# Convolution taps as diagonal matmuls, four norms scaled on VectorE, a split last FFN, and a new instruction order

## The chip, the cores and the metric

The kernel runs on 1 core of one Trainium2 chip. The metric is the device time of one execution in microseconds (us). Matmuls are TensorE (PE), elementwise work and reductions are VectorE (DVE), activations and copies are ScalarE (ACT), small elementwise work and masks are GpSimd (POOL); SyncE (SP) issues all DMAs.

## What is computed

One pre-norm decoder layer over 8 sequences of 256 tokens with 128 channels, in float32:

```python
x = x + linear_attention(layernorm(x), Wqkv, Wproj) + bproj     # 16 heads of 8, elu+1 feature map
x = x + causal_softmax_attention(layernorm(x), ctx, Wq, Wk, Wv, Wo)
x = x + ffn(layernorm(x))
# ffn(h): scores = sigmoid(h @ Wr); top 2 of 8 experts, weights cw normalised
#   experts 0..3: (silu(h@Wg) * (h@Wu)) @ Wd;  4 and 6: h;  7: relu(h);  5: nothing
#   routed = sum of cw * expert;  shared = causal depthwise convolution of h over 4 tokens + conv_b
#   return routed + shared
```

## The kernel before

Each of the 8 sequences is a "batch" of 256 tokens, held as two token tiles of 128 (T = 2). A batch passes through three stages. The self stage (names `self_*`, `xn`, `phiq`, `kvsum`, `o`) ends in `x1`. The cross stage builds three bfloat16 parts each of q and k, sends them by DMA into stacked tiles `qs` and `ks`, finds the row maxima (`max`, six units for a batch, each read by one DVE `reduce` of 128x1024), then computes the scores again (`soft`), exponentiates them on ACT (`exp`), masks on POOL and multiplies by the values (`pv`); it ends in `x2`. The FFN stage normalises (`norm3`), transposes (`ffn_x_t`), routes (`route`, ten small DVE instructions), multiplies by gate and up (`ffn_gate_up`), forms the hidden values (`gate`, `times_up` on DVE, `hid` on POOL), transposes them (`ffn_hid_t`), copies them (`hidT` on ACT), and multiplies by down (`ffn_down`); `finish` on DVE adds `base` and `store_out` writes 128 KB.

A layer norm goes through three engines: DVE computes mean and variance (`stats`, `var`, L686 and L697), POOL computes `vareps`, `negmean`, `rstd` and `shift` (L488 to L497, four instructions), and ACT writes `xn = x * rstd + shift`, one instruction for each token tile (L565).

The convolution has four taps. POOL computes the last one with its bias (`conv`, L529); DVE adds the other three (`tap`, L840, 128x256 each, both inputs in SBUF); `ffn_down` adds the sum on PE with one matmul by the identity for each token tile.

The order of all work is written out by hand: a table `ORDER` gives for each engine a list of words `step.batch.argument`, and every engine runs its list strictly in that order, waiting on semaphores. Stages of several batches are interleaved in it: around one word of batch 7's softmax stand words of the FFN of batches 4 and 5. `BANKS` says which PSUM bank each stay uses. `warm.b.n` puts n float32 128x128 matmuls by the identity on PE whose result nobody reads; 18 more stand at the start. Nineteen such matmuls stand in the PE list after the last `max` words. `clear` (eight DVE memsets of 128x1024) prepares `ks` and `qs`; `heads`, `causal`, `picks` and others on POOL prepare constants.

## Time and profile before

| | |
|---|---|
| time, median of 3 runs | 182.6 us (182.4 to 182.61) |
| the profiled execution | 182.75 us, of which its span, first to last instruction, is 181.0 us |
| busy: PE / DVE / ACT / POOL | 94% / 89% / 71% / 65% of the span |
| DVE reductions of the scores | 48 of 1.22 us, from 30.3 to 143.7 us |
| last result written by DVE, end of the span | 178.7 us, 181.0 us |
| granted TensorE clock | 1.00 in every stretch |

Read it in three stretches. Until 30 us the self stage of the first batches runs and the constants are made. From 30 to 144 us the reductions run, six for a batch. From 144 us on only softmax, `pv` and the FFNs of the last batches are left; the time ends with batch 7's store. A matmul's duration in the trace contains its pipeline, so successive matmuls overlap, and the distance from start to start says more than the duration. One float32 matmul stands as two records.

### The profile page before, as it was taken

How to read it: one execution, taken by the hardware profiler on the slowest of the kernel's cores; microseconds unless marked ns; L12 is line 12 of the kernel's file. 1: busy time of each engine (PE TensorE's matmuls, PEld its weight loads, DVE VectorE, ACT ScalarE, POOL GpSimd, SP SyncE). 2: the span in 40 equal slices, each digit the busy share in tenths (PEclk: the TensorE clock that was granted, in tenths of full speed). 3: DMA queues.
4: the chain of work that ended last, by engine and by line, in shares of the span. 5: the costliest groups of instructions: out<-in, count | busy, mean ns of one | idle time of the engine just before them, and what ended most of it. 6: DMA issues, size and time to landing. Idle time of an engine off the chain costs nothing. (4 is left out here: it accounts for less than half of the span.)

```text
span 181.0 us, 5282 instructions
## 1 busy us (share of the span) xinstructions
PE 169.6 (94%) x1898; PEld 119.3 (66%) x1898; DVE 160.6 (89%) x448; ACT 127.8 (71%) x289; POOL 118.3 (65%) x248
## 2 busy tenths in 40 slices
PE   6889999989999999999999999989989899999993
PEld 6856788757666767656765687457646647756593
DVE  6897789999997998899999998999799879979992
ACT  1469988687788958977978679488564878663540
POOL 6768887764686757758846358468457577757541
DMA  5781023311323122123322122142000010000001
GB/s 175 222 320 41 5 61 81 89 50 45 78 61 91 40 55 63 46 59 81 85 57 63 33 51 71 38 107 87 2 4 0 5 31 4 2 29 4 29 2 58
...
## 3 DMA queue, kind: packets, MB, share of 16 engines
...
q14 instruction: 10, 0.08, 0.2%
...
## 5 line engine op out<-in xcount | busy, mean ns | idle before, releaser
L752 DVE TENSOR_REDUCE negmax<-max_pair 128x4 f32<-128x1024 f32 (+1 forms) x48 | 58.4, 1217 | 4.3 <-PE max_pair L862 3.8
L622 ACT ACTIVATE probs<-soft_pair 128x1024 f32<-128x1024 f32 x48 | 49.3, 1026 | 12.9 <-PE soft_pair L862 12.7
L521 POOL TENSOR_SCALAR_AFFINE_SELECT probs<-probs 128x512 f32<-128x512 f32 (+1 forms) x48 | 37.6, 796 | 15.6 <-ACT probs L622 15.6
L862 PE MATMUL pv_bank<-probs,vs 128*32 128x256 f32 (+1 forms) x448 | 21.1, 329 | 0.1
L862 PE MATMUL soft_pair<-qs,ks 64*128 64x256 bf16 (+1 forms) x256 | 18.8, 245 | 0.4 <-DMA qs<-maxparts 0.3
L536 POOL TENSOR_TENSOR hid<-hraw,cw 128x256 f32<-128x256 f32 x16 | 10.5, 661 | 12.9 <-DVE cw L806 10.7
L495 POOL TENSOR_TENSOR rstd<-vareps,exponent 128x2 f32<-128x2 f32 x24 | 17.5, 728 | 2.0
L862 PE MATMUL max_pair<-ks,qs 64*128 64x128 bf16 (+1 forms) x256 | 18.4, 242 | 0.0
L862 PEld LDWEIGHTS pv_bank<-probs,vs 128*32 128x32 f32 x448 | 12.8, 109 | 7.2 <-issue 1.7
L862 PE MATMUL max_pair<-causal,picks 64*128 64x128 bf16 (+1 forms) x192 | 15.2, 237 | 1.6 <-DVE negmax L752 0.8
L565 ACT ACTIVATE xn<-inputs,shift,rstd 128x128 f32<-128x128 f32 x32 | 14.1, 492 | 3.1 <-POOL shift L497 3.1
L862 PE MATMUL ffn_bank<-inputs,x3T 128*128 128x8 f32 (+1 forms) x46 | 15.3, 429 | 0.0
L862 PEld LDWEIGHTS soft_pair<-qs,ks 64*128 64x128 bf16 x256 | 8.2, 94 | 9.8 <-ACT probs L622 4.0
L840 DVE SCALAR_TENSOR_TENSOR conv<-x3T,inputs,conv 128x256 f32<-128x256 f32 x24 | 14.4, 602 | 0.1
L862 PE MATMUL max_pair<-ident 128*128 128x128 f32 x74 | 12.1, 315 | 1.6 <-POOL ident L416 1.6
L862 PEld LDWEIGHTS max_pair<-causal,picks 64*128 64x128 bf16 x192 | 6.6, 94 | 8.3 <-DVE negmax L752 4.6
L862 PEld LDWEIGHTS max_pair<-ident 128*128 128x128 f32 x74 | 11.0, 227 | 1.6 <-POOL ident L416 1.6
L862 PE MATMUL cross_bank<-inputs 128*128 128x128 f32 (+1 forms) x48 | 10.9, 336 | 0.6 <-DVE krest L741 0.6
L488 POOL TENSOR_SCALAR vareps<-mv 128x2 f32<-128x2 f32 x24 | 5.1, 211 | 8.3 <-DVE mv L697 7.0
L862 PEld LDWEIGHTS max_pair<-ks,qs 64*128 64x128 bf16 x256 | 9.8, 94 | 0.4
L547 POOL TENSOR_TENSOR base<-skip,relu 128x256 f32<-128x256 f32 x8 | 5.8, 726 | 5.2 <-DVE skip L832 4.9
L862 PEld LDWEIGHTS cross_bank<-inputs 128*128 128x128 f32 x48 | 6.7, 190 | 2.6 <-issue 1.1
...
## 6 DMA issues: line engine op xcount, KB each, us to landing
...
qs<-maxparts SPq DMA_DIRECT2D x32, 4.0 KB
...
```

The source lines that it names most:

```text
L488: nc.gpsimd.tensor_scalar(t["vareps"][:, :], t["mv"][b.par][:, :, 1], 1.0, 1e-5, ALU.mult, ALU.add).then_inc(vareps_done[n], 1)
L495: nc.gpsimd.tensor_tensor(t["rstd"][b.par][:, :], t["vareps"][:, :], exponent[:, :], ALU.pow).then_inc(rstd_done[n], 1)
L521: nc.gpsimd.affine_select(out=v, in_=v, compare_op=ALU.is_ge, fill=0.0, base=0, pattern=[[0, n], [1, P]], channel_multiplier=-1).then_inc( ...
L536: nc.gpsimd.tensor_tensor(hid[b.par][:, t, :].rearrange("p (e i) -> p e i", e=EM), hid0[:, t, :].rearrange("p (e i) -> p e i", e=EM), cw[b ...
L547: nc.gpsimd.tensor_tensor(base[b.par][:, :, :], skip[b.par][:, :, :], relu7[b.par][:, :, :], ALU.add).then_inc(base_done, 1)
L565: nc.scalar.activation(t["out"][b.par][:, i, :], source(n, b)[:, i, :], ACT.Identity, scale=t["rstd"][b.par][:, i:i + 1], bias=t["shift"][ ...
L622: nc.scalar.activation(probs[b.par][g][:, k, :], soft_pair[:, :], ACT.Exp).then_inc(exp_done, 1)
L752: nc.vector.tensor_reduce(maxima, max_pair[:, :].rearrange("p (u h k) -> p u h k", u=2, h=n), AX.X, ALU.max, negate=True).then_inc(max_rea ...
L840: nc.vector.scalar_tensor_tensor(out=conv[b.par][:, :], in0=x3T[b.par][:, j:j + S], scalar=w["conv"][:, j:j + 1], in1=conv[b.par][:, :], o ...
L862: return nc.tensor.matmul(out, lhsT, rhs, start=start, stop=stop, skip_group_check=True)
```

## The change

1. **Norms on DVE.** For norm 1 of batches 0 and 1 and norm 3 of batches 6 and 7, POOL computes only `vareps` and `rstd`, and DVE writes `xn = (x - mean) * rstd`, two instructions of 128x128 (`centre`). ACT's two instructions go away for them.
2. **Taps on PE.** For batches 6 and 7 the three DVE taps go away. ACT makes three diagonal matrices once (`diagonals`), and `ffn_conv` puts for each token tile one matmul by the identity and three by the diagonals on PE, ahead of `ffn_down`, into the bank of down's result.
3. **The last FFN by token tile.** For batch 7 `ffn_hid_t`, `hidT`, `ffn_down`, `finish` and `store_out` run once for each token tile, in banks of their own.
4. **Another order.** The lists of all five engines are rearranged. 8 `warm` matmuls instead of 19 stand at the end of PE's list, and 4 new ones stand in its beginning. On SP the two loads of the router bias move from behind `lo_q.0.0` to ahead of `lo_k.0.0`.
5. A few waits are added or moved (`act_q` waits for `phiq` two batches back, `x2` for `skip` two batches back).

```diff
+XN_ON_VECTOR = {1: (0,1), 2: (), 3: (6, 7)}
+LAST = B - 1
+CONV_ON_PE = (6, 7)
 ORDER = {
...
-        self_x_t.0.0 self_q1.0.0 cross_k.0.0 self_kv.0.0 self_x_t.1.0 cross_v.0.0 self_sum.0.0 self_q1.1.0 self_out.0.0
+        self_x_t.0.0 self_q1.0.0 warm.0.1 cross_k.0.0 warm.0.1 self_kv.0.0 cross_v.0.0 self_x_t.1.0 self_sum.0.0
...
-    "cross_bank": "cross.0 cross.1 cross.2 cross.3 cross.4 cross.5 cross.6 cross.7 pv.6",
+    "cross_bank": "cross.0 cross.1 cross.2 cross.3 cross.4 cross.5 cross.6 cross.7 pv.6 down.6",
-    "soft_high": "self.4 soft.all up.6",
+    "soft_high": "self.4 soft.all up.6 downb.7",
-    "max_high": "max.all",
+    "max_high": "max.all down.7",
...
                 def go(b, _):
+                    direct = b.c in XN_ON_VECTOR[n]
                     pool.wait_ge(mv_done[n], b.count(2, 2))
...
-                    nc.gpsimd.tensor_scalar(t["negmean"][:, :], t["mv"][b.par][:, :, 0], -1.0, 0.0,
-                                            ALU.mult, ALU.add).then_inc(vareps_done[n], 1)
+                    if not direct:
+                        nc.gpsimd.tensor_scalar(t["negmean"][:, :], t["mv"][b.par][:, :, 0], -1.0, 0.0,
+                                                ALU.mult, ALU.add).then_inc(vareps_done[n], 1)
...
+                    if direct:
+                        return
...
+            def centre(n):
+                t = norm[n]
+
+                def go(b, _):
+                    dve.wait_ge(rstd_done[n], b.count(1, 1))
...
+                    for i in range(T):
+                        nc.vector.scalar_tensor_tensor(out=t["out"][b.par][:, i, :], in0=source(n, b)[:, i, :],
+                                                       scalar=t["mv"][b.par][:, i, 0:1],
+                                                       in1=t["rstd"][b.par][:, i:i + 1].to_broadcast([P, C]),
+                                                       op0=ALU.subtract, op1=ALU.mult).then_inc(xn_done[n], 1)
...
+            def spread_taps(_, __):
...
+                for j in range(KC - 1):
+                    nc.scalar.activation(diagonals[:, j, :], ident[:, :], ACT.Identity, scale=w["conv"][:, j:j + 1]).then_inc(diagonals_done, 1)
...
+            def ffn_conv(b, _):
...
+                for t in range(T):
+                    o = half_down(b, t)
+                    mm(o, conv[b.par][:, t * P:(t + 1) * P], ident[:, :], start=t == 0 or b.c == LAST, stop=False)
+                    for j in range(KC - 1):
+                        mm(o, x3T[b.par][:, j + t * P:j + (t + 1) * P], diagonals[:, j, :], start=False, stop=False)
+
+            def ffn_down(b, half):
+                pe.wait_ge(hidT_done, b.count(1, half + 1))
...
+                for t in [half] if b.c == LAST else range(T):
+                    o = half_down(b, t)
                     for i in range(2):
...
-            def finish(b, _):
+            def finish(b, t):
...
+                if b.c == LAST:
+                    nc.vector.tensor_tensor(result[b.par][:, t, :], half_down(b, t), base[b.par][:, t, :], ALU.add).then_inc(result_done, 1)
+                    return
```

Lines of the changed kernel are higher by some 30 to 90: L734 there is L686 before (`stats`), L747 is L697 (`var`), L721 is L673 (`clear`), L880 and L887 are L813 and L820 (`gate`, `times_up`), L905 is L840 (`tap`), L852 to L873 are L785 to L806 (`route`), L931 is L862 (matmuls), L1142 and L1148 are L1073 (`ffn_hid_t`), and L759 is `centre`.

DVE at the start, from the first statistics to the feature map of batch 0. Before:

```order
L686 BN_STATS stats1<-inputs 128x6 x2
L697 BN_AGGR mv1_0<-stats1 128x2 x2
L686 BN_STATS stats1<-inputs 128x6 x2
L697 BN_AGGR mv1_1<-stats1 128x2 x2
L673 MEMSET qs1 128x1024
L673 MEMSET ks2 128x1024
...
L741 SCALAR_TENSOR_TENSOR krest0<-cross_bank,kparts0 128x256
L703 SCALAR_TENSOR_TENSOR phiq0<-expq0,reluq0 128x256
L708 SCALAR_TENSOR_TENSOR phik0<-expk0,reluk0 128x256
```

Now:

```order
L734 BN_STATS stats1<-inputs 128x6 x2
L721 MEMSET qs1 128x1024
L747 BN_AGGR mv1_0<-stats1 128x2 x2
L721 MEMSET ks2 128x1024
L734 BN_STATS stats1<-inputs 128x6 x2
L759 SCALAR_TENSOR_TENSOR xn1_0<-inputs,mv1_0,rstd1_0 128x128 x2
L721 MEMSET qs2 128x1024
...
L806 SCALAR_TENSOR_TENSOR krest0<-cross_bank,kparts0 128x256
L747 BN_AGGR mv1_0<-stats1 128x2 x2
L759 SCALAR_TENSOR_TENSOR xn1_1<-inputs,mv1_1,rstd1_1 128x128 x2
L773 SCALAR_TENSOR_TENSOR phik0<-expk0,reluk0 128x256
```

One memset of 128x1024 now stands between the statistics and the variance of batch 0, one more before batch 1's statistics, and the two pairs that write `xn` stand among them; `phiq0` now comes later, before `kvsum0`.

DVE after the last statistics of batch 5, where batch 4 meets its gate. Before:

```order
L774 TENSOR_TENSOR x2_1<-pv_bank,inputs 128x256
L686 BN_STATS stats3<-x2_1 128x6 x2
L697 BN_AGGR mv3_1<-stats3 128x2 x2
L757 TENSOR_TENSOR maxparts1<-soft_pair,maxparts1 16x128
L813 SCALAR_TENSOR_TENSOR gated<-tang,ffn_bank 128x256
L785 SCALAR_TENSOR_TENSOR biased<-tanr0,rbias_all 128x2x8
L820 SCALAR_TENSOR_TENSOR hraw<-gated,ffn_bank 128x256
```

Now:

```order
L841 TENSOR_TENSOR x2_1<-pv_bank,inputs 128x256
L734 BN_STATS stats3<-x2_1 128x6 x2
L747 BN_AGGR mv3_1<-stats3 128x2 x2
L822 TENSOR_TENSOR maxparts1<-soft_pair,maxparts1 16x128
L852 SCALAR_TENSOR_TENSOR biased<-tanr0,rbias_all 128x2x8
L905 SCALAR_TENSOR_TENSOR conv0<-x3T0,inputs,conv0 128x256
L858 MAX best<-biased 128x8 x2
L880 SCALAR_TENSOR_TENSOR gated<-tang,ffn_bank 128x256
```

Three steps that do not need ACT's `tang` now stand ahead of the one that does.

DVE from the `x2` of batch 7 (`x2_1`) to the weights of batch 6. Before:

```order
L774 TENSOR_TENSOR x2_1<-pv_bank,inputs 128x256
L793 COPY match<-best 128x2x2
L686 BN_STATS stats3<-x2_1 128x6 x2
L697 BN_AGGR mv3_1<-stats3 128x2 x2
L813 SCALAR_TENSOR_TENSOR gated<-tang,ffn_bank 128x256
L840 SCALAR_TENSOR_TENSOR conv0<-x3T0,inputs,conv0 128x256 x2
L796 MATCH_REPLACE picked<-match,biased 128x14 x2
L820 SCALAR_TENSOR_TENSOR hraw<-gated,ffn_bank 128x256
```

Now:

```order
L841 TENSOR_TENSOR x2_1<-pv_bank,inputs 128x256
L734 BN_STATS stats3<-x2_1 128x6 x2
L747 BN_AGGR mv3_1<-stats3 128x2 x2
L880 SCALAR_TENSOR_TENSOR gated<-tang,ffn_bank 128x256
L852 SCALAR_TENSOR_TENSOR biased<-tanr0,rbias_all 128x2x8
L858 MAX best<-biased 128x8 x2
L860 COPY match<-best 128x2x2
L887 SCALAR_TENSOR_TENSOR hraw<-gated,ffn_bank 128x256
L759 SCALAR_TENSOR_TENSOR xn3_1<-x2_1,mv3_1,rstd3_1 128x128 x2
```

The taps are gone, routing of batch 6 has moved behind `x2_1`, and the norm of batch 7 is written here.

PE from the hidden transposes of batch 6 to the end. Before:

```order
L1073 MATMUL ffn_bank<-ident,hid0 128x128 x4
L862 MATMUL max_pair<-ident 128x128 x3
L862 MATMUL ffn_bank<-inputs,hidT0 128x128 x2
L862 MATMUL ffn_bank<-ident,conv0 128x128
...
L862 MATMUL max_pair<-ident 128x128
L1073 MATMUL max_pair<-ident,hid1 128x128 x4
L862 MATMUL max_pair<-ident 128x128 x5
L862 MATMUL max_pair<-inputs,hidT1 128x128 x2
L862 MATMUL max_pair<-ident,conv1 128x128
```

Now:

```order
L1148 MATMUL ffn_bank<-ident,hid0 128x128 x4
L931 MATMUL cross_bank<-ident,conv0 128x128
L931 MATMUL cross_bank<-diagonals,x3T0 128x128 x3
...
L931 MATMUL cross_bank<-inputs,hidT0 128x128 x4
L1142 MATMUL max_pair<-ident,hid1 128x128 x2
L931 MATMUL max_pair<-ident,conv1 128x128
L931 MATMUL max_pair<-diagonals,x3T1 128x128 x3
L931 MATMUL soft_pair<-ident,conv1 128x128
L931 MATMUL soft_pair<-diagonals,x3T1 128x128 x3
L1142 MATMUL soft_pair<-ident,hid1 128x128 x2
L931 MATMUL max_pair<-inputs,hidT1 128x128 x2
L931 MATMUL soft_pair<-inputs,hidT1 128x128 x2
```

The nine warm matmuls of this stretch have gone, and 16 matmuls of the convolution stand in it (4 of the old form went away).

## Rows read from the trace of the kernel before

**Rows 1.** The page's busy time: us, share of the span, instructions.
```profile
PE 169.6 (94%) x1898; PEld 119.3 (66%) x1898; DVE 160.6 (89%) x448; ACT 127.8 (71%) x289; POOL 118.3 (65%) x248
```

**Rows 2.** Windows: stretch, length, busy of PE, PEld, DVE, ACT, POOL, clock, DMA, GB/s.
```profile
0.00:13.00 13.00, 10.03 (x55) 8.61 (x55) 10.58 (x25) 5.42 (x13) 8.85 (x37) 1.00 0.73 245
13.00:30.00 17.00, 16.32 (x108) 13.36 (x108) 14.02 (x62) 15.13 (x47) 14.09 (x36) 1.00 0.17 43
30.00:150.00 120.00, 116.05 (x1517) 77.31 (x1512) 110.69 (x269) 92.05 (x196) 77.97 (x147) 1.00 0.21 54
165.00:181.00 16.00, 12.72 (x86) 10.00 (x84) 11.77 (x46) 5.67 (x15) 7.39 (x14) 1.00 0.08 26
```

**Rows 3.** Timeline, VectorE, start: start, us, instruction, idle before it.
```profile
5.79 0.91 DVE L673 MEMSET qs<- 128x1024 f32 x1 [0.16 <-DVE mv L697]
...
12.18 0.42 DVE L708 SCALAR_TENSOR_TENSOR phik<-expk,reluk 128x256 f32<-128x256 f32 x1
...
13.44 0.31 DVE L716 TENSOR_TENSOR kvsum<-self_bank,headmask 128x144 f32<-128x144 f32 x1 [0.17 <-PE self_bank L862]
```

**Rows 4.** Timeline, ScalarE and PE at the start, VectorE's first reduction.
```profile
6.40 0.88 ACT L565 ACTIVATE xn<-inputs,shift,rstd 128x128 f32<-128x128 f32 x2 [1.13 <-POOL shift L497]
...
7.63 0.38 PE L866 MATMUL self_bank<-ident,xn 128*128 128x128 f32 x2
...
30.29 1.23 DVE L752 TENSOR_REDUCE negmax<-max_pair 128x8 f32<-128x1024 f32 x1
```

**Rows 5.** Timeline, VectorE, the four long waits between 50 and 150 us.
```profile
56.25 1.23 DVE L752 TENSOR_REDUCE negmax<-max_pair 128x8 f32<-128x1024 f32 x1 [1.14 <-PE max_pair L862]
...
110.25 0.24 DVE L785 SCALAR_TENSOR_TENSOR biased<-tanr,rbias_all 128x16 f32<-128x16 f32 x1 [0.73 <-ACT tanr L644]
...
129.50 0.42 DVE L774 TENSOR_TENSOR x<-pv_bank,inputs 128x256 f32<-128x256 f32 x1 [0.67 <-PE pv_bank L862]
...
146.56 0.42 DVE L813 SCALAR_TENSOR_TENSOR gated<-tang,ffn_bank 128x256 f32<-128x256 f32 x1 [0.91 <-ACT tang L649]
```

**Rows 6.** The chain that ended last, batch 7's norm: start, us, what.
```profile
165.37 0.19 POOL vareps L488
...
165.65 0.42 POOL negmean L490
...
166.14 0.94 POOL rstd L495
...
167.16 0.20 POOL shift L497
...
167.39 0.89 ACT xn L565 x2
...
168.32 0.45 PE max_pair L866 x2
```

**Rows 7.** Timeline, PE and VectorE's last instruction, batches 6 and 7 to the end.
```profile
171.92 0.60 PE L1073 MATMUL ffn_bank<-ident,hid 128*128 128x128 f32 x4
...
173.20 0.71 PE L862 MATMUL ffn_bank<-inputs,hidT 128*128 128x128 f32 x4
...
174.64 0.39 PE L862 MATMUL max_pair<-ident 128*128 128x128 f32 x2
...
176.62 0.68 PE L862 MATMUL max_pair<-inputs,hidT 128*128 128x128 f32 x4
...
178.28 0.42 DVE L848 TENSOR_TENSOR result<-max_pair,base 128x256 f32<-128x256 f32 x1 [0.96 <-PE max_pair L862]
```

**Rows 8.** Taps and skips on VectorE: count, ns min/median/max, first and last start.
```profile
L840 DVE SCALAR_TENSOR_TENSOR conv<-x3T,inputs,conv x24: 446/480/1178, 83.2 to 176.0; 128x256 f32<-128x256 f32 x24
...
L832 DVE SCALAR_TENSOR_TENSOR skip<-xn,cskip,x x16: 327/344/779, 87.8 to 177.0; 128x128 f32<-128x128 f32 x16
```

**Rows 9.** Timeline, POOL and VectorE side by side in the tail.
```profile
174.94 0.72 POOL L547 TENSOR_TENSOR base<-skip,relu 128x256 f32<-128x256 f32 x1 [0.55 <-DVE skip L832]
174.98 1.49 DVE L840 SCALAR_TENSOR_TENSOR conv<-x3T,inputs,conv 128x256 f32<-128x256 f32 x2
```

305 lines of the change are left out of this document (174 added, 131 removed).

## The prediction

> **What bounds the kernel now.** I read the page's busy times first, then windows for three stretches, then the timeline around the waits, then the chain that ended last. The page [rows 1] shows PE at 94% and DVE at 89% of the span. A PE duration contains its pipeline, so PE's share overstates it; DVE's does not. The windows [rows 2] show where DVE has room: 2.4 us idle of 13 at the start, 3.0 of 17 from 13 to 30 us, 9.3 of 120 from 30 to 150 us, 4.2 of 16 at the end. So from 30 to 150 us DVE is busy 92% of the time, with 48 reductions among it that each need PE's scores first, and what counts there is how well two nearly full engines mesh. The largest single DVE waits of that stretch are four [rows 5]: 1.14, 0.73, 0.67 and 0.91 us, together 3.45 us, a third of the idle 9.3. In each of them DVE stands at an instruction whose input is late while others behind it could run. The end is another thing: the chain [rows 6] runs through batch 7's norm, from POOL's `vareps` at 165.37 to PE's transpose at 168.32 us, then through PE and DVE to `result` [rows 7]. The last result is written at 178.28 + 0.42 = 178.70 us and the span ends at 181.0, so the store takes 2.3 us, and 1.7 us of the 182.75 lie outside the span. The sum below is made against 182.75; the median of the runs shown is 182.6, 0.15 less, and I take 0.15 off at the end.
>
> **The start: late by 0.5 us (a gain of 0.3 to a loss of 1.3).** The norms of batches 0 and 1 leave ACT. What goes: POOL's `negmean` and `shift` (0.2 us each, as `shift` in [rows 6], with some 0.1 of hand-over each) and a pair on ACT of 0.88 [rows 4]. What comes: a pair on DVE of 128x128 with both inputs in SBUF. No such pair by that name exists before; the nearest row is `skip`, 0.33 at least, 0.34 in the median, 0.78 at most [rows 8], so a pair is 0.65 to 1.56, and 0.7 where POOL is quiet. Taken alone batch 0 would gain 0.6 + 0.2 = 0.8. But the order puts one memset of 0.91 plus 0.16 [rows 3] ahead of the variance of batch 0 and another ahead of `centre`. `xn` of batch 0 was done at 6.40 + 0.88 = 7.28 and PE took it at 7.63, behind its 18 warm matmuls [rows 4]. Now: variance one memset later, 4.75 + 1.07 = 5.8; `vareps` and `rstd` 1.1; `centre` waits for its place on DVE, behind the second memset and batch 1's statistics (5.8 + 1.1 + 0.5 = 7.4), and ends at 8.1. PE takes it at some 8.1 in place of 7.63: 0.5 late. Then DVE has, ahead of `kvsum` of batch 0, two pairs (1.4) more, and no wait of 0.17: on DVE alone `kvsum` (13.44 in [rows 3]) would be 1.3 late. Part of this is work that stood behind it anyway, and the 3.0 us that DVE idles from 13 to 30 us [rows 2] can take it up; but the chain of batch 0 to the first reduction at 30.29 [rows 4] is one of latencies, and most of its 0.5 stays. I take +0.5, the delay that PE sees first; 1.3 is DVE's whole delay, passed on; -0.3 is the case that batch 0 is late only where it would have waited later anyway and the reordered SP list pays (the two router loads now issue where SP waits for `lo_k`). The four new warm matmuls cost nothing as long as PE waits there for ACT; without that cover each is 0.26 (five in 1.32 us would be so by [rows 7], where they fill the gap up to 176.62), 1.0 in all, within the 1.3.
>
> **The middle: 0.9 us gained (3.0 gained to 1.5 lost).** The work stays the same: no instruction of the loops goes or comes but three short ACT instructions that make the diagonals, where ACT is busy 92.05 of 120 us [rows 2]; they hide there, and cost 3 x 0.44 (half of a pair in [rows 4]) if they do not. What changes is the order. At all four waits of [rows 5] other steps now stand ahead: the remainder of k for batch 4 and `x1` of batch 6 ahead of the reduction at 56.25; two taps of batch 2 ahead of `biased` at 110.25; two small steps of routing ahead of `x` at 129.50; routing, one tap and MAX ahead of `gated` at 146.56 (the second place shown). By size that is 0.8, 0.73, 0.3 to 0.67 and 0.9: up to 3.0 us. A filled hole pays only if DVE is what the next hole waits for, and every moved word opens holes that the trace of before cannot show. That PE is hardly ever idle either says that part of the time filled on DVE is spent waiting again later. I take a third, 0.9. The bounds are all of it, and half of it as a loss.
>
> **The end: 0.7 us gained (1.6 gained to 0.3 lost).** Batch 7's norm [rows 6]: `x2` of batch 7 waits for PE, as before. Variance is done at 165.29. Before, from there to `xn`'s end at 168.28 it takes 3.0. Now: hand-over and `vareps` 0.27; hand-over 0.08 and `rstd`, which took 0.94 here because a tap stood beside it, 0.70 or 0.94; `centre`'s pair 0.7, behind gate and three routing steps that are ready and short, with 0.05: 1.8 to 2.1, or 167.3. PE's matmuls of batch 5's down end there too. So PE's transpose starts 0.95 earlier, at 167.37. If the centre pair costs 1.56 it is 0.1 to 0.35 earlier; if nothing but the pair counted, 1.2.
> From there PE has one fixed list. Before, it went from the hidden transposes of batch 6 at 171.92 to the end of `result` at 178.70 in 6.8 us, nine of its matmuls being warm [rows 7]. Now, from 170.97: four transposes 0.44; a float32 matmul takes (174.64 - 173.20) / 6 = 0.24 from start to start [rows 7]; 8 of the convolution 1.92, 4 of down 0.96, two transposes 0.22, 8 of the convolution 1.92, two transposes 0.22, in sum 176.65; then ACT's copy of half the hidden values with its hand-overs 0.6 (down of the first tile runs under it, 0.48); two matmuls 0.48 and 0.15 to drain; `result` of one tile 0.3: 178.2. That is 0.5 before the 178.70, and 0.95 at 0.22 for a matmul, the smallest distance that down shows: I take 0.7. So PE gives back a part of what the norm wins: 16 matmuls in the place of 4 and 9 warm ones, but DVE, which must not be late, now has room. The six taps of batches 6 and 7 cost DVE some 3.4 us (six of the 24 in [rows 8], two of them the 1.49 of [rows 9]) and the two pairs bring 1.4; base and hidden values of batch 7 are needed by 176.1 and due near 175. If they were late by 1.0, the end would be a loss of 0.3. The store of half the size starts once its tile is done; SP's issue of the first half is over by then. I leave the 2.3 as they are, with no gain for the smaller size.
>
> **A rule weighed.** The taps have both inputs in SBUF. Beside a tap, POOL's `negmean` took 0.42 where `vareps` took 0.19 [rows 6], and beside POOL's `base` two taps took 1.49 where their median gives 0.96 [rows 8, 9]. The Trainium skill, page "SBUF — State Buffer", section "Who interferes with whom", says that a DVE instruction with two SBUF inputs contends with a GpSimd instruction that reads SBUF, and the later one waits for the earlier one to finish. The trace agrees. By that rule the change takes six such instructions away but makes the eight instructions of `centre` ones of the same kind, and ACT's form of the norm had no such trouble; what it would do is the rival "centre blocked" below.
>
> **The rivals.**
> *The holes were DVE's own.* DVE is the bound of the middle, and all 3.0 us come back. For it: 92% busy, and each hole has ready work behind it. Against: PE's idle is as small, and such gains seldom add up. 182.75 + 0.5 - 3.0 - 0.7 - 0.15 = 179.4 us.
> *Late start, slower.* The memsets and pairs ahead of batch 0's variance and `kvsum` push the whole chain, 1.3 us, into the first reduction, and the middle, full to 92%, cannot catch up. It decides if the first reduction starts later than some 31.3 in place of 30.29; with new holes as large as those filled the time is 182.75 + 1.3 - 0.7 - 0.15 = 183.2 us. For it: DVE has no wait from 5.8 to 13.4 us, so each added instruction there moves all behind it. Against: 3.0 us of room from 13 to 30 us.
> *Nothing in sum.* The middle gives 0, the start costs 0.5 and the end gives 0.7: 182.4 us, within what can be told from no change.
> *Centre blocked.* The pair of batch 7 meets POOL's `conv` and `base` (0.72 in [rows 9]) and takes 1.4 to 1.56: `xn` 0.85 later than I have it, the end gains 0.1 only. 182.75 + 0.5 - 0.9 - 0.1 - 0.15 = 182.1 us.
>
> **How the numbers follow.** Forecast: 182.75 + 0.5 - 0.9 - 0.7 - 0.15 = 181.5 us. Chances: forecast 0.42 (its own range 180.5 to 182.2), holes 0.14, centre blocked 0.10, nothing 0.14, late start 0.20. The sum of the terms' bounds would reach from 177.7 to 185.7, but they will hardly fall together. I take 179.6 to 183.2: it leaves out half of the first rival and half of the late start, 0.17. A measurement of this kernel can tell about 0.2% (0.37 us) from no change. Faster: 0.42 + 0.14 + 0.10 = 0.66. Same: 0.14. Slower: 0.20.
>
> **What would show it right or wrong.** The first reduction starts at 30.8, not at 30.3 or 31.6. `xn` of batch 0 ends near 8.1. DVE's waits at batch 2's first reduction, batch 2's routing, batch 4's gate and batch 4's `x2` shrink to under 0.4 each, and its idle time from first to last reduction drops by about 1. The last reduction is over 0.4 earlier than 143.7. From the variance of batch 7 to PE's transpose it takes 2.1 us, not 3.0. The 16 convolution matmuls stand 0.22 to 0.26 apart, and PE runs without a gap from the hidden transposes of batch 6 to those of batch 7. The prediction is wrong if batch 7's hidden values reach PE after 176.1, if `centre` takes over 0.5 us for one instruction, or if the DVE waits of the middle only change their place.

## The result, and the profile after

The changed kernel takes 183.24 us (median of 5 runs, 183.13 to 183.51), the kernel before, measured beside it, 182.44 us (182.4 to 182.61). The ratio is 1.0036, 95% interval 1.0025 to 1.0046: **slower by 0.8 us** between the medians, where 181.5 and "faster" were forecast. The interval is clear of noise, and the difference is small, 0.25% to 0.46%. The profiled execution took 183.24 us with a span of 181.2; before it was 182.75 and 181.0. So 0.2 us more stand inside that span, and 2.0 us instead of 1.7 outside it. The profiled span of before is 0.1 to 0.3 above what later executions of it mostly show (180.7 to 180.9), so the loss inside the span is nearer to 0.5, the 0.8 less the 0.3 outside.

Busy times of the page after, against [rows 1]; under it groups of DVE's instructions (count, busy time, mean ns of one, idle time before them and who ended it), against [rows 8]:

```profile
PE 169.7 (94%) x1908; PEld 119.9 (66%) x1908; DVE 160.6 (89%) x451; ACT 126.4 (70%) x285; POOL 117.7 (65%) x240
```

```profile
L817 DVE TENSOR_REDUCE negmax<-max_pair 128x4 f32<-128x1024 f32 (+1 forms) x48 | 58.4, 1217 | 5.2 <-PE max_pair L931 4.9
L905 DVE SCALAR_TENSOR_TENSOR conv<-x3T,inputs,conv 128x256 f32<-128x256 f32 x18 | 12.6, 698 | 0.7 <-POOL conv L561 0.6
...
L852 DVE SCALAR_TENSOR_TENSOR biased<-tanr,rbias_all 128x16 f32<-128x16 f32 x8 | 3.8, 470 | 0.3 <-ACT tanr L680 0.2
...
L759 DVE SCALAR_TENSOR_TENSOR xn<-x,mv,rstd 128x128 f32<-128x128 f32 x4 | 1.4, 376 | 0.0
```

DVE is as busy as before, though six taps left it and only eight short `centre` instructions came. The 24 taps had taken 602 ns each, the 18 take 698; `biased` went from 351 to 470 ns. The same work has become longer. The next two views show the stretch that has grown. The windows from the start of the first reduction to the end of the last (stretch, its length, DVE's busy time and instructions, granted clock, DMA share, GB/s), first of before, then of after:

```profile
30.29:143.69 113.40, 105.83 (x249) 1.00 0.22 56
```

```profile
30.56:145.60 115.04, 107.02 (x252) 1.00 0.21 55
```

This stretch has grown by 1.64 us, 1.19 of it busy and 0.45 idle (7.57 before, 8.02 after). No work was meant to be added to it, though the new order moves three instructions into it (an `x2`, a reciprocal and a small addition, some 0.9 us together), and elsewhere in it copies and skips have become shorter by some 1.4 us. What has grown most is the twelve taps of the stretch (7.3 to 8.5 us) and its four `biased` (1.0 to 2.3). Most of that growth stands in one place, the second hole of [rows 5], at 110 us, where two taps of batch 2 now stand ahead of `biased`. The timeline after, DVE, POOL and PE:

```profile
109.00 1.20 DVE L817 TENSOR_REDUCE negmax<-max_pair 128x4 f32<-128x1024 f32 x1
110.38 1.77 DVE L905 SCALAR_TENSOR_TENSOR conv<-x3T,inputs,conv 128x256 f32<-128x256 f32 x2 [0.17 <-POOL conv L561]
112.07 1.06 DVE L852 SCALAR_TENSOR_TENSOR biased<-tanr,rbias_all 128x16 f32<-128x16 f32 x1
113.05 1.21 DVE L817 TENSOR_REDUCE negmax<-max_pair 128x4 f32<-128x1024 f32 x1
```

```profile
109.78 0.56 POOL L561 TENSOR_SCALAR conv<-x3T,inputs 128x256 f32<-128x256 f32 x1 [1.85 <-ACT x3T L676]
110.30 0.64 POOL L553 TENSOR_SCALAR_AFFINE_SELECT probs<-probs 128x512 f32<-128x512 f32 x1
...
111.24 3.04 POOL L553 TENSOR_SCALAR_AFFINE_SELECT probs<-probs 128x512 f32<-128x512 f32 x4
```

```profile
114.31 0.39 PE L931 MATMUL max_pair<-causal,picks 64*128 64x256 bf16 x4 [1.49 <-DVE negmax L817]
```

The hole of 0.73 us is gone, and in its place stand 0.17 of waiting for POOL's part of the convolution, 1.77 for two taps, and 1.06 for a `biased` of 128x16 that takes 0.17 where it is left alone. From the end of one reduction to the start of the next it is 2.85 us. The reduction of unit 5 of batch 5 starts at 113.05; it started at 110.68. PE, which waits for that reduction before its next scores, idles 1.49 us in one piece.

### The profile page after: what moved, and what is told of

It reads as the page before. It is cut to its first block, busy times and chain, and to the rows that moved or that the text cites. A ratio compares the mean times of both kernels' runs of the same rounds, so it can differ in the third digit from the quotient of the medians.

```text
span 181.2 us, 5300 instructions
## 1 busy us (share of the span) xinstructions
PE 169.7 (94%) x1908; PEld 119.9 (66%) x1908; DVE 160.6 (89%) x451; ACT 126.4 (70%) x285; POOL 117.7 (65%) x240
## 3 DMA queue, kind: packets, MB, share of 16 engines
HBM read 3.10 MB, written 1.05 MB: 23 GB/s over the span
## 4 chain that ended last, share of the span: by engine, by line
PE 56%; DVE 20%; POOL 9%; issue 8%; ACT 6%; POOLq 0%; DVEq 0%
PE soft_pair L931 11%; PE max_pair L931 10%; PE ffn_bank L931 9%; PE pv_bank L931 9%; PE cross_bank L931 6%; DVE negmax L817 5%; PE self_bank L931 4%; ACT probs L658 3%; DVE conv L905 3%; POOL probs L553 2%; POOL rstd L525 2%; DVE qs L721 2%; DVE ks L721 2%; PE ffn_bank L1148 1%; PE ffn_bank L935 1%
## 5 line engine op out<-in xcount | busy, mean ns | idle before, releaser
L553 POOL TENSOR_SCALAR_AFFINE_SELECT probs<-probs 128x512 f32<-128x512 f32 (+1 forms) x48 | 38.2, 803 | 22.9 <-ACT probs L658 22.7
L931 PE MATMUL pv_bank<-probs,vs 128*32 128x256 f32 (+1 forms) x448 | 21.1, 329 | 0.0
L931 PE MATMUL soft_pair<-qs,ks 64*128 64x256 bf16 (+1 forms) x256 | 18.8, 245 | 0.3
L931 PE MATMUL max_pair<-ks,qs 64*128 64x128 bf16 (+1 forms) x256 | 18.4, 242 | 0.0
L568 POOL TENSOR_TENSOR hid<-hraw,cw 128x256 f32<-128x256 f32 x16 | 9.9, 622 | 12.3 <-DVE cw L873 10.0
L931 PEld LDWEIGHTS pv_bank<-probs,vs 128*32 128x32 f32 x448 | 12.7, 109 | 7.2 <-issue 1.9
L931 PE MATMUL max_pair<-causal,picks 64*128 64x128 bf16 (+1 forms) x192 | 15.3, 237 | 2.2 <-DVE negmax L817 1.9
L931 PE MATMUL ffn_bank<-inputs,x3T 128*128 128x8 f32 (+1 forms) x46 | 15.5, 433 | 0.0
L931 PEld LDWEIGHTS soft_pair<-qs,ks 64*128 64x128 bf16 x256 | 8.2, 94 | 8.2 <-issue 4.0
L905 DVE SCALAR_TENSOR_TENSOR conv<-x3T,inputs,conv 128x256 f32<-128x256 f32 x18 | 12.6, 698 | 0.7 <-POOL conv L561 0.6
L931 PEld LDWEIGHTS max_pair<-causal,picks 64*128 64x128 bf16 x192 | 6.4, 94 | 10.1 <-DVE negmax L817 6.2
L599 ACT ACTIVATE xn<-inputs,shift,rstd 128x128 f32<-128x128 f32 x28 | 12.2, 489 | 0.9 <-POOL shift L529 0.9
L931 PE MATMUL max_pair<-ident 128*128 128x128 f32 x60 | 10.1, 318 | 1.6 <-POOL ident L443 1.6
L931 PE MATMUL cross_bank<-inputs 128*128 128x128 f32 (+1 forms) x48 | 10.5, 327 | 0.5 <-DVE krest L806 0.5
L931 PEld LDWEIGHTS max_pair<-ident 128*128 128x128 f32 x60 | 9.2, 229 | 1.9 <-POOL ident L443 1.6
L931 PEld LDWEIGHTS max_pair<-ks,qs 64*128 64x128 bf16 x256 | 9.9, 94 | 0.3
L931 PEld LDWEIGHTS cross_bank<-inputs 128*128 128x128 f32 x48 | 6.7, 190 | 2.0 <-DVE krest L806 0.9
L931 PEld LDWEIGHTS ffn_bank<-inputs,x3T 128*128 128x128 f32 x46 | 6.5, 189 | 2.2 <-issue 1.3
```

The source lines that it names most:

```text
L553: nc.gpsimd.affine_select(out=v, in_=v, compare_op=ALU.is_ge, fill=0.0, base=0, pattern=[[0, n], [1, P]], channel_multiplier=-1).then_inc( ...
L568: nc.gpsimd.tensor_tensor(hid[b.par][:, t, :].rearrange("p (e i) -> p e i", e=EM), hid0[:, t, :].rearrange("p (e i) -> p e i", e=EM), cw[b ...
L599: nc.scalar.activation(t["out"][b.par][:, i, :], source(n, b)[:, i, :], ACT.Identity, scale=t["rstd"][b.par][:, i:i + 1], bias=t["shift"][ ...
L905: nc.vector.scalar_tensor_tensor(out=conv[b.par][:, :], in0=x3T[b.par][:, j:j + S], scalar=w["conv"][:, j:j + 1], in1=conv[b.par][:, :], o ...
L931: return nc.tensor.matmul(out, lhsT, rhs, start=start, stop=stop, skip_group_check=True)
```

## The experiments

**Theory A**: the loss is made between the start and the last reduction, by DVE's new places for taps. **Rival B**: the late start grows on its own. **Rival C**: the end makes it, with sixteen matmuls more and a split FFN. **Rival E**: lateness in the middle is absorbed at the end, and the end wins nothing.

The order table makes it possible to join one kernel's list up to an instant to the other's remaining words. In every joined kernel all engines change lists at the same instant of the traces: at 40 us (on DVE behind the fifth reduction), at 96 us (ahead of the last reduction of batch 4), or behind the last reduction. They keep the wait of the kernel before in `skip`, and so do e5, e11, e15 and e18 below, which are the changed kernel otherwise; it is a wait of DVE for its own earlier instructions.

### One stretch at a time

```diff
 e1_middle:    before up to 40 us | changed | before from behind reduce.7.5   (computation as before)
 e2_end:       before up to reduce.7.5 | changed
+XN_ON_VECTOR = {1: (), 2: (), 3: (6, 7)}; CONV_ON_PE = (6, 7); last FFN split
-  dve: var3.7.0 gate.6.0 tap.6.0 tap.6.1 route.6.3 times_up.6.0 route.6.4 tap.6.2 ...
+  dve: var3.7.0 gate.6.0 route.6.0 route.6.1 route.6.2 times_up.6.0 centre3.7.0 route.6.3 ...
 e3_start:     changed up to 40 us | before
+XN_ON_VECTOR = {1: (0, 1), 2: (), 3: ()}
 e4_start_end: changed up to 40 us | before up to reduce.7.5 | changed
```

> Only the middle of the new order: the computation, the start (up to the fifth reduction of batch 0, 40 us) and the end (behind the last reduction of batch 7) are those of the kernel before, and between them all five engines run the changed kernel's lists. Theory A (the middle makes the loss: DVE's new places for taps cost more than the holes they fill): the last reduction starts 1.3 to 1.9 us later than 142.46 and the time is 183.4 to 184.2 us. Rival B (the late start of 0.3 us grows on its own): last reduction within 0.5 us of before, 182.3 to 182.8 us. Rival C (the end makes the loss: matmuls of the convolution and the split FFN): 182.3 to 182.8 us as well. Rival E (a late middle is absorbed, since PE has other work at the end): the last reduction late by 1.3 or more, but the time 182.4 to 182.9 us.

> Only the end of the change: the kernel before up to the last reduction of batch 7, from there the changed kernel's lists with norm 3 of batches 6 and 7 on DVE, the convolution of both on PE and the split last FFN; the diagonals are made on ACT in the middle. Theory A: the last reduction is where it was and the end gains, 181.2 to 182.0 us. Rival C: 182.9 to 183.3 us. Rival E (what the end seemed to win back in the changed kernel was only the lateness that was absorbed): 182.1 to 182.5 us.

> Only the start of the change: norm 1 of batches 0 and 1 on DVE and the changed kernel's lists up to 40 us, then the kernel before. Theory A: the first reduction starts 0.27 late, and what is left of it at the end is 0 to 0.3 us: 182.4 to 182.8 us. Rival B: the delay carries through and grows, 183.0 us or more.

> The changed kernel with only its middle taken back: start and end as changed, the order between 40 us and the last reduction that of the kernel before. Theory A: all of the middle's loss goes and the end's gain stays, 181.3 to 182.1 us, faster than both kernels. Rival B: 182.9 to 183.2 us. Rival C: 183.0 to 183.4 us. Rival E: 182.3 to 182.7 us.

| kernel | us, median | before beside it | ratio, 95% interval | start of the last reduction (142.46 before, 144.37 changed) |
|---|---|---|---|---|
| e1_middle | 183.87 | 182.54 | 1.0069 (1.0051 to 1.0086) | 144.42 |
| e2_end | 181.54 | 182.54 | 0.9946 (0.9926 to 0.9965) | 142.20 |
| e3_start | 183.24 | 182.54 | 1.0032 (1.0019 to 1.0045) | 143.11 |
| e4_start_end | 182.76 | 182.54 | 1.0006 (0.9995 to 1.0017) | 142.84 |

e1 and e2 came out as theory A had them (the last reduction of e1, 1.96 us late, is just outside its 1.3 to 1.9), and C and E fall: the middle by itself loses 1.3 us, the end by itself wins 1.0, and the lateness of e1's last reduction is still 1.12 at the last result. e2_end beats both kernels. B as the only cause falls by e1. But A missed in the other two: e3, at 183.24, lies where B had it, and e4, at 182.76, is 0.7 above A's range and in nobody's. e1, e3 and e4 carry a cost of the joint: there the reduction behind 40 us is set back by 0.3 to 0.4 us at once, though in e1 the start is that of before. So these three overstate, and what the start costs is not settled by them.

### The middle: two words

```diff
 e5_taps_back (changed kernel, dve):
-  reduce.5.4 tap.2.0 tap.2.1 route.2.0 reduce.5.5 route.2.1 x2.3.0 route.2.2 route.2.3 reduce.6.0 ... times_up.2.1 reduce.6.3
+  reduce.5.4 route.2.0 reduce.5.5 route.2.1 x2.3.0 route.2.2 route.2.3 tap.2.0 reduce.6.0 ... times_up.2.1 tap.2.1 reduce.6.3
 e6_taps_ahead (kernel before, dve):
-  reduce.5.4 route.2.0 route.2.1 reduce.5.5 route.2.2 route.2.3 tap.2.0 x2.3.0 ... times_up.2.1 tap.2.1
+  reduce.5.4 tap.2.0 tap.2.1 route.2.0 route.2.1 reduce.5.5 route.2.2 route.2.3 x2.3.0 ... times_up.2.1
 e7_late_half: before up to 96 us | changed | before from behind reduce.7.5
 e18_three_back (e5, and the last tap of batch 1 back as well):
-  route.1.3 tap.1.2 reduce.5.0 ... reduce.5.2
+  route.1.3 reduce.5.0 ... reduce.5.2 tap.1.2
```

> The changed kernel with two words of DVE's list moved back to where they stand before: the first two taps of batch 2, from ahead of batch 2's first routing step and its neighbour, the reduction of unit 5 of batch 5, to behind that reduction and behind the second hidden product. Theory F (the two taps fill a wait of 0.73 us, but stand beside POOL's masks, take 1.8 us instead of 0.9, and push a reduction for which PE waits): the reduction of unit 5 of batch 5 starts 1.0 to 1.8 us earlier than 113.05 and the time is 182.0 to 182.7 us (0.5 to 1.2 less than 183.24). Rival G (the loss of the middle lies in PE's and POOL's rearranged lists, the taps only show it): 183.0 to 183.5 us.

> The kernel before with just these two words moved the other way: both taps of batch 2 ahead of its first routing step, in the wait of 0.73 us at 110.25. Theory F: DVE's wait is gone, the two taps take 1.4 to 1.8 us there, the next reduction starts 0.7 to 1.2 us late and the time is 183.0 to 183.7 us. Rival H (the wait was DVE's own, filling it pays): 181.8 to 182.3 us. Rival G: 182.4 to 182.7 us.

> As e1_middle, but the changed kernel's lists only from 96 us (the reduction of unit 5 of batch 4) to the last reduction; everything else is the kernel before. e1_middle lost 1.3 us in all. Theory F: nearly all of it is made here, 183.3 to 183.9 us. Rival (it is made evenly, a bit at every moved word, or at the seam of e1_middle at 40 us): 182.8 to 183.2 us.

> e5_taps_back with one more tap back where it stood: the last tap of batch 1 from ahead of the first reduction of batch 5 to behind its third. In the changed kernel that reduction started 1.44 us later than before, the next 0.5 less. If such a tap costs as the two of batch 2 did: 0.3 to 0.6 less than e5_taps_back's 182.42. If the lateness is made good by the next reductions, as the rows of the changed kernel show: within 0.15 of it, 182.3 to 182.55 us.

e5_taps_back: 182.42 us (before 182.57; ratio 0.999, 0.998 to 1.0001), 0.8 less than the changed kernel. Its reduction of unit 5 of batch 5 starts at 111.38, 1.67 us earlier, and 1.13 of that is left at the last one. e6_taps_ahead: 183.11 us (182.57; 1.0028, 1.0018 to 1.0038). Two words make the loss of 0.5 us in the kernel before and of 0.8 in the changed one: F holds in both times, G and H fall; the next reduction of e6 is 1.64 us late, more than the 0.7 to 1.2 that F had. e7_late_half: 183.42 us (182.57; 1.0047, 1.003 to 1.0065), at the lower edge of F's range; of the middle's 1.3 some 0.85 shows here, with whatever its own joint costs. e18: 182.44 (182.66; 0.9986, 0.9976 to 0.9995). The third tap costs nothing. It made its own reduction 0.78 us late (99.59, here 98.81), and three reductions later that was made good. Being late once is not the loss; being late beyond what the others have in reserve is. e5 also says how large the middle is. With only these two words taken back it is 0.34 us faster than e4_start_end, in which the whole middle is taken back (and which carries the joint). So the two words are the greater part of what the middle loses, and nothing here shows that the rest of it loses anything. The 1.03 us that DVE waits ahead of the last reduction of the changed kernel stand in e5 as well (1.04).

### Why two taps cost more than their hole: wait or contention

Four fills for the same hole of the kernel before, ahead of `route.2.0`. Besides e6's taps there are two memsets or two instructions of the taps' form, all into a tile that nobody reads, with or without the taps' wait for POOL's part of the convolution.

```diff
 e12_fill_unread, e17_fill_wait, e13_fill_two_inputs (kernel before, dve):
-  reduce.5.4 route.2.0
+  reduce.5.4 fill.2.0 fill.2.1 route.2.0
+            def fill(b, i):
+                dve.wait_ge(conv_begun, b.count(1, 1))                                  # e17 alone
+                nc.vector.memset(unread[:, 512 * i:512 * i + 512], 0.0)                 # e12, e17
+                nc.vector.scalar_tensor_tensor(out=unread[:, i, :], in0=w["qkv"][:, 0:S], scalar=w["conv"][:, i:i + 1],
+                                               in1=w["qkv"][:, C:C + S], op0=ALU.mult, op1=ALU.add)   # e13
```

> The kernel before with two memsets of 128x512 (0.47 us each) to a tile that nobody reads, at the place where e6_taps_ahead has the two taps (two taps are 0.99 us where POOL is quiet, 0.84 + 0.77 there). Nothing else moves. Theory C (what e6 lost is contention: both inputs of a tap in SBUF beside POOL's masks, and `biased` behind them too): the memsets take 0.94 to 1.1 us, the next reduction starts 0.2 to 0.4 us later than 110.68 and the time is 182.4 to 182.8 us. Rival (a reduction for which PE waits is late by whatever stands in front of it, contention or not): the reduction late by 0.6 or more, 182.9 to 183.2 us.

> e12_fill_unread, but in place of the two memsets two instructions of a tap's form (128x256 out, two float32 inputs of 128x256 in SBUF), from weights that were loaded long before, into the tile that nobody reads: they wait for nobody. e6_taps_ahead's taps also waited 0.39 us for POOL's part of the convolution, which these don't. If the two inputs in SBUF beside POOL are what costs: each takes 0.7 to 0.9 us in place of 0.5, the next reduction starts 0.3 to 1.0 us later than e12's 110.53, and the time is 182.7 to 183.1 us. If the wait for POOL's part was the cost: 182.4 to 182.6 us as e12.

> e12_fill_unread with the wait of the taps: each memset waits for POOL's part of batch 2's convolution first, as the taps of e6_taps_ahead do. So the wait is there and the contention of two SBUF inputs is not. By the rows of e6 and e13 the wait alone moves the fill from 109.28 to some 109.97 and the next reduction from 110.53 to 111.3; with the contention e6 had it at 112.32. If the wait makes the loss: reduction at 111.2 to 111.5 and 182.8 to 183.1 us. If wait and contention both are needed (the reduction has some slack before PE is held): 182.4 to 182.7 us.

| | fill: start, both take | next reduction (110.68 before) | us (before beside it) |
|---|---|---|---|
| memsets, no wait (e12) | 109.28, 1.02 | 110.53 | 182.42 (182.50) |
| two inputs, no wait (e13) | 109.25, 0.86 | 110.42 | 182.35 (182.59) |
| memsets, wait (e17) | 109.91, 1.03 | 111.19 | 182.51 (182.66) |
| two inputs, wait: the taps (e6) | 109.97, 1.65 | 112.32 | 183.11 (182.57) |

The timelines that the table is from, DVE and POOL of e6_taps_ahead:

```profile
109.97 1.65 DVE L906 SCALAR_TENSOR_TENSOR conv<-x3T,inputs,conv 128x256 f32<-128x256 f32 x2 [0.39 <-POOL conv L560]
111.54 0.60 DVE L851 SCALAR_TENSOR_TENSOR biased<-tanr,rbias_all 128x16 f32<-128x16 f32 x1
...
112.32 1.21 DVE L816 TENSOR_REDUCE negmax<-max_pair 128x4 f32<-128x1024 f32 x1
```

```profile
109.88 0.65 POOL L552 TENSOR_SCALAR_AFFINE_SELECT probs<-probs 128x512 f32<-128x512 f32 x1
110.49 0.84 POOL L542 TENSOR_TENSOR kparts<-krest,kparts 128x256 bf16<-128x256 f32 x1
```

and of e13_fill_two_inputs:

```profile
109.25 0.86 DVE L923 SCALAR_TENSOR_TENSOR unread<-inputs 128x256 f32<-128x256 f32 x2
...
110.42 1.21 DVE L818 TENSOR_REDUCE negmax<-max_pair 128x4 f32<-128x1024 f32 x1
```

```profile
109.11 1.47 POOL L562 TENSOR_SCALAR conv<-x3T,inputs 128x256 f32<-128x256 f32 x1 [2.09 <-ACT x3T L677]
```

and DVE of e12_fill_unread and of e17_fill_wait:

```profile
109.28 1.02 DVE L923 MEMSET unread<- 128x512 f32 x2
...
110.53 1.21 DVE L818 TENSOR_REDUCE negmax<-max_pair 128x4 f32<-128x1024 f32 x1
```

```profile
109.91 1.03 DVE L924 MEMSET unread<- 128x512 f32 x2 [0.52 <-POOL conv L562]
...
111.19 1.21 DVE L818 TENSOR_REDUCE negmax<-max_pair 128x4 f32<-128x1024 f32 x1
```

Neither cause alone costs time. A reduction that is 0.5 us late (e17) is absorbed, because PE has other work until then: it comes to the next scores at 112.32 us in the kernel before and at 112.45 in e17. In e6 it comes to them at 113.59, after waiting 1.05 us for the reduction. PE of e6, then of e17:

```profile
113.59 0.39 PE L932 MATMUL max_pair<-causal,picks 64*128 64x256 bf16 x4 [1.05 <-DVE negmax L816]
```

```profile
112.45 0.39 PE L938 MATMUL max_pair<-causal,picks 64*128 64x256 bf16 x4
```

The contention is there in e13 too, but POOL pays it, 1.47 us for an instruction of 0.56, and POOL has time. Where the taps first wait for POOL, they start while its next instruction is under way, and then DVE pays: 1.65 for two instead of 0.86, and 0.60 for `biased` instead of some 0.17. With the later start this is 1.64 us in sum, beyond what is absorbed. The Trainium skill, page "SBUF — State Buffer", section "Who interferes with whom", says that the order of issue decides who is blocked. e6 agrees: the mask on POOL starts at 109.88 and the taps at 109.97. In e13 the records do not bear it out: POOL's `conv` starts at 109.11 and DVE's pair at 109.25, and yet POOL is the one that is held. 0.14 us may be finer than these records show, so who was first there stays open; that POOL paid is measured.

Behind the reduction DVE makes up time as well. The small copy `match` took 0.96 us there in the kernel before, and 0.82, 0.30 and 0.31 in e12, e13 and e17; why it was shorter was not tested. Before, then e17:

```profile
111.80 0.96 DVE L793 COPY match<-best 128x4 f32<-128x4 f32 x1
```

```profile
112.31 0.31 DVE L861 COPY match<-best 128x4 f32<-128x4 f32 x1
```

The comparison is not exact: e6 moves work and the fills add some, which makes the fills' result the stronger; the fills' inputs are other tiles than a tap's.

### The end: norm, convolution, split

```diff
 e8_norm_only (kernel before, norm 3 of batches 6 and 7 on DVE):
-  dve: times_up.5.0 route.5.7 ... gate.6.0 tap.6.0 tap.6.1 route.6.3 times_up.6.0 route.6.4
+  dve: times_up.5.0 centre3.6.0 route.5.7 ... gate.6.0 route.6.3 times_up.6.0 centre3.7.0 tap.6.0 tap.6.1 route.6.4
 e9_end_no_norm (e2_end):
-XN_ON_VECTOR = {1: (), 2: (), 3: (6, 7)}
+XN_ON_VECTOR = {1: (), 2: (), 3: ()}
+  act: outT.7.0 norm3.6.0 tanh_g.5.1 ... tanh_g.6.1 norm3.7.0 x3T.7.0
 e10_end_no_split (e2_end, pe):
-  ffn_hid_t.7.0 ffn_conv.7.0 ffn_hid_t.7.1 ffn_down.7.0 ffn_down.7.1
+  ffn_hid_t.7.0 ffn_conv.7.0 ffn_down.7.0
 e16_conv_ahead (e10, pe):
-  ffn_hid_t.7.0 ffn_conv.7.0 ffn_down.7.0
+  ffn_conv.7.0 ffn_hid_t.7.0 ffn_down.7.0
```

> The kernel before with norm 3 of batches 6 and 7 scaled on DVE and nothing else: taps, one last FFN and warm matmuls as before. e2_end won 1.0 us. If the norm wins it: from the variance of batch 7 to PE's transpose 1.9 to 2.2 us in place of 3.3, and 181.3 to 181.9 us. If the convolution on PE and the split FFN are needed (DVE has the taps and the pairs, and hidden values of batch 7 come late): 182.1 to 182.6 us.

> e2_end with norm 3 of batches 6 and 7 on POOL and ACT as before; the convolution on PE and the split last FFN stay. e2_end was 1.0 us faster than before, e8_norm_only (the norm alone, with DVE's taps left in) was 2.7 us slower. If the norm makes e2_end's gain once DVE is rid of the taps: PE's transpose of batch 7 starts 0.8 to 1.2 us later than e2_end's 167.13, and the time is 182.3 to 182.9 us. If the convolution on PE makes it: 181.4 to 181.9 us.

> e2_end with the last FFN in one piece (hidden transposes, their copy, down, result and store of batch 7 once for both token tiles); norm on DVE and convolution on PE stay. If the split pays, by the copy of half the hidden values and the store of half the size: 181.9 to 182.4 us, 0.4 to 0.8 more than e2_end. If it is nothing: 181.4 to 181.7 us.

> e10_end_no_split (183.14 us) with one word of PE's list moved: the eight matmuls of batch 7's convolution ahead of its hidden transposes, where PE waits for POOL, not behind them. If the split's 1.6 us were mostly that the convolution fell on the path behind the hidden values: 182.0 to 182.5 us. If the split itself makes it (copy, down, result and store of half the size): 182.8 to 183.1 us.

| kernel | us (before beside it) | ratio, 95% interval |
|---|---|---|
| e2_end: norm, convolution, split | 181.54 (182.54) | 0.9946 (0.9926 to 0.9965) |
| e9: without the norm | 182.29 (182.50) | 0.9986 (0.9975 to 0.9996) |
| e10: without the split | 183.14 (182.50) | 1.0027 (1.0015 to 1.0038) |
| e16: without the split, convolution ahead | 182.53 (182.59) | 0.9996 (0.9982 to 1.0011) |
| e8: norm alone | 185.24 (182.57) | 1.0137 (1.0114 to 1.0159) |

The norm on DVE is worth 0.75 us, and PE's transpose of batch 7 moves from 167.72 (e9) to 167.13 (e2), 0.59 where 0.8 to 1.2 were expected. The split is worth 1.6 us, twice what was expected at most; 0.6 of it is order (e16), and 1.0 is left for the split itself. Without it all the hidden values of batch 7 must be there before PE can begin, and what is behind them is a chain of whole-batch pieces. PE of e10, then of e16:

```profile
175.32 0.66 PE L1149 MATMUL max_pair<-ident,hid 128*128 128x128 f32 x4 [0.95 <-POOL hid L567]
175.81 0.39 PE L932 MATMUL max_pair<-ident,conv 128*128 128x128 f32 x2
...
177.60 1.06 PE L932 MATMUL max_pair<-inputs,hidT 128*128 128x128 f32 x8
```

```profile
175.54 0.60 PE L1149 MATMUL max_pair<-ident,hid 128*128 128x128 f32 x4
176.81 1.16 PE L932 MATMUL max_pair<-inputs,hidT 128*128 128x128 f32 x8 [0.68 <-ACT hidT L706]
```

In e10 PE idles 0.95 and then does the eight convolution matmuls that could have stood there. In e16 it waits 0.68 for the copy of all hidden values, and then has four matmuls of down ahead of the result, where e2 has two. The norm alone (e8) loses 2.7 us, far outside both of its ranges. The taps are still on DVE. The loss begins at the norm of batch 6, whose pair waits 0.54 us for POOL and takes 0.61: the variance of batch 7 ends at 166.32 in place of 165.29. Then the pair of batch 7 stands beside POOL's `base` and takes 1.08, and the last tap is late for PE. DVE, POOL and PE of e8, for batch 7:

```profile
167.41 1.08 DVE L759 SCALAR_TENSOR_TENSOR xn<-x,mv,rstd 128x128 f32<-128x128 f32 x2 [0.17 <-POOL rstd L525]
```

```profile
167.52 0.83 POOL L579 TENSOR_TENSOR base<-skip,relu 128x256 f32<-128x256 f32 x1
```

```profile
177.89 0.68 PE L933 MATMUL max_pair<-inputs,hidT 128*128 128x128 f32 x4 [0.40 <-DVE conv L907]
```

The profiled execution took 184.31 us, the fastest of six, so its rows can account for at most 1.7 of the 2.7 us. The others reach to 185.5, and the rest stays open.

### The start, and the time outside the span

```diff
 e11_back_no_warm (e5_taps_back, pe): the words warm.0.1 warm.0.1 warm.0.2 taken out
 e14_start_to_31: as e3_start, but changed up to 31.5 us, behind the first reduction | before
 e15_pool_pad (e5_taps_back, pool):
-  base.4.0 hid.5.0
+  base.4.0 pad.0.0 pad.0.1 pad.0.2 pad.0.3 hid.5.0          (four memsets of 128x1)
```

> e5_taps_back without the four new warm matmuls in the beginning of PE's list (128x128 float32, 8 records). In all kernels with start and end of the change the measured time is 2.0 us more than the span, in all others 1.7. Theory P (it hangs on the number of PE's instructions): 1.7 here and, the span as in e5_taps_back, 182.1 us. Rival (it hangs on POOL's or another engine's program, or on something else): still 2.0 and 182.3 to 182.5 us. Were the warm matmuls a cost of the start, the first reduction would be 0.2 us or more earlier than 30.56.

> e3_start with the seam at 31.5 us, just behind the first reduction, in place of 40 us, where e3's second and later reductions were set back by 0.3 us more (e1_middle's as well, with the start of the kernel before: a cost of the seam). If the start costs what the first reduction shows, 0.27 to 0.41: 182.7 to 183.0 us. If it costs what e3 showed in all: 183.1 to 183.3 us. If it costs nothing by itself: 182.4 to 182.6 us.

> e5_taps_back with four memsets of one column on POOL, to a tile that nobody reads, behind batch 4's `base` where POOL idles 3.0 us. All kernels that measure 2.0 us more than their span have 322 instructions of all kinds on POOL in the trace, all others 326 or more. If the difference hangs on POOL's program: 1.7 here, and 182.1 us. If not: 2.0 and 182.3 to 182.5 us.

e11: 182.30 us (182.50), 2.0 outside the span; theory P falls, and the warm matmuls cost nothing that can be told. e14: 183.46 us (182.59), more than e3: its second reduction is 1.47 us late where the first was 0.34. The joint costs more than the start, and the experiment does not separate them; it missed all three of its ranges. A better measure of the start is the first reduction in the profiles at hand: with the start of before it begins at 30.26 to 30.79 (12 profiles, median 30.32), with the changed start at 30.56 to 30.82 (8 profiles, median 30.66). So the start sets the first reduction back by 0.3 us, with a scatter of the same size. Whether it costs more later is not shown: e3 lost 0.7 us, its joint included. e15: 182.40 us (182.59), and 1.8 to 1.9 outside the span in all 11 runs, while the span grew. POOL's program has a part in it, but nothing is won.

## Why the prediction was wrong, step by step

The changes of the parts were forecast as +0.5 (start), -0.9 (middle), -0.7 (end); the runs give some +0.3 to +0.7 for the start, +0.8 to +1.2 for the middle, -1.0 for the end, and +0.3 outside the span. The split between start and middle is open. The first value of the start is the first reduction's delay, the second e3 with its joint; the two words alone make 0.8 of the middle (e5), late half and joint 0.85 (e7), and +1.2 is what a start of +0.3 would leave. In every case the sign of the middle was wrong, and its error of 1.7 us or more is the largest.

**The middle: the step that failed.** "By size that is 0.8, 0.73, 0.3 to 0.67 and 0.9: up to 3.0 us" took the size of a hole for the gain and never asked what the filler takes in it. Two taps were due there, 0.96 us by the median of [rows 8], and up to 1.49 beside POOL by [rows 9]; their wait for POOL was in the diff. With 1.77 + 0.17 in the place of 0.73, the next reduction is over 1 us late, before `biased` is counted, and e5 and e6 show what that costs: 0.8 us in the changed kernel and 0.5 in the one before. The rule on two SBUF inputs was weighed in the prediction, but for `centre`, where it did no harm (376 ns of one after, the median of `skip` being 344 before), and not for the taps, which the new order moved next to POOL's masks. The upper bound of 1.5 us for a loss in the middle held. "The DVE waits only change their place" was named as what would make it wrong, and in sum it holds. All four waits shrank to under 0.4 us, as forecast, but others came. At 56.25 us 1.14 became 0.33, and one reduction earlier stand 0.82 that were not there. At 146.56 the 0.91 ahead of `gated` are gone, and earlier, ahead of the last reduction, stand 1.03 (0.27 before):

```profile
54.16 1.22 DVE L817 TENSOR_REDUCE negmax<-max_pair 128x4 f32<-128x1024 f32 x1 [0.82 <-PE max_pair L931]
...
56.52 1.23 DVE L817 TENSOR_REDUCE negmax<-max_pair 128x8 f32<-128x1024 f32 x1 [0.33 <-PE max_pair L931]
```

```profile
144.37 1.23 DVE L817 TENSOR_REDUCE negmax<-max_pair 128x4 f32<-128x1024 f32 x1 [1.03 <-PE max_pair L931]
```

DVE's idle time between first and last reduction was to drop by 1 us; it rose by 0.45. The last reduction was to be over 0.4 us earlier; it is 1.91 later.

**The start: right in sign, by another way.** The +0.5 was "the delay that PE sees first", and that delay is nothing. `xn` of batch 0 ends at 7.57, not 8.1: statistics and variances slip in between the memsets more closely than the sum had it. PE takes it at 7.62, as before (7.63). `kvsum` is at 13.45, as before (13.44), against a delay of DVE put at up to 1.3 us. DVE, then PE:

```profile
5.46 0.18 DVE L747 BATCH_NORM_AGGREGATE mv<-stats 128x2 f32<-128x6 f32 x2
...
6.97 0.60 DVE L759 SCALAR_TENSOR_TENSOR xn<-inputs,mv,rstd 128x128 f32<-128x128 f32 x2
...
13.45 0.30 DVE L781 TENSOR_TENSOR kvsum<-self_bank,headmask 128x144 f32<-128x144 f32 x1
```

```profile
7.62 0.44 PE L935 MATMUL self_bank<-ident,xn 128*128 128x128 f32 x2
```

The first reduction is at 30.56, against 30.8. In PE's list a delay first shows later, at a norm that kept its old form: its `shift` on POOL ends at 13.66 (13.43 before), and PE's transpose behind it starts at 14.62 (14.40). Whether this is what sets back the first reduction is not shown. The rival "late start", which was to decide from 31.3 on, is not what happened, though its time, 183.2 us, is the one measured: the right side for the wrong reason.

**The end: the norm was right, and two things in the split were not in the sum.** From the variance of batch 7 to PE's transpose it is 1.92 us (2.1 forecast, 3.03 before). Engines of the changed kernel against [rows 6], then PE and DVE against [rows 7]:

```profile
166.41 0.25 DVE L747 BATCH_NORM_AGGREGATE mv<-stats 128x2 f32<-128x6 f32 x2
...
166.74 0.19 POOL L517 TENSOR_SCALAR vareps<-mv 128x2 f32<-128x2 f32 x1 [1.35 <-DVE mv L747]
...
167.77 0.75 DVE L759 SCALAR_TENSOR_TENSOR xn<-x,mv,rstd 128x128 f32<-128x128 f32 x2
...
168.58 0.44 PE L935 MATMUL max_pair<-ident,xn 128*128 128x128 f32 x2
```

```profile
172.18 0.60 PE L1148 MATMUL ffn_bank<-ident,hid 128*128 128x128 f32 x4
...
175.52 0.39 PE L931 MATMUL max_pair<-ident,conv 128*128 128x128 f32 x2
...
177.30 0.38 PE L1142 MATMUL soft_pair<-ident,hid 128*128 128x128 f32 x2
177.52 0.61 PE L931 MATMUL max_pair<-inputs,hidT 128*128 128x128 f32 x4
178.15 0.71 PE L931 MATMUL soft_pair<-inputs,hidT 128*128 128x128 f32 x4
```

```profile
178.17 0.29 DVE L914 TENSOR_TENSOR result<-max_pair,base 128x128 f32<-128x128 f32 x1 [1.33 <-PE max_pair L931]
178.90 0.29 DVE L914 TENSOR_TENSOR result<-soft_pair,base 128x128 f32<-128x128 f32 x1 [0.43 <-PE soft_pair L931]
```

Eight convolution matmuls take 1.78 us (175.52 to 177.30), 0.22 from start to start, as said, and PE has no gap. From the hidden transposes of batch 6 to the end of the last result it is 7.01 us here; 7.23 were forecast (170.97 to 178.2) and 6.78 measured before. In e2_end the gain is 1.0 against the 0.7 of the sum. In its profile the last reduction is 0.26 us earlier than before and the last result 0.97, so 0.7 up to the result is as forecast. The other 0.3 is the store: the span ends 2.0 us behind the last result, where the sum left the 2.3. The split was costed only as a shorter drain. e10 and e16 show that it carries 1.6 us: without it norm and convolution together would have lost 0.6 (e10), or won nothing (e16, with the convolution put ahead).

**Outside the span.** The prediction took the 1.7 us as fixed. The kernels with both the changed start and the changed end (the changed one, e4, e5, e11, e18) have 2.0, e15 has 1.8 to 1.9, and all others have 1.7, in every run. This 0.3 is over a third of the measured loss.
